# Reordering GpSimd's deviations, gathers and scatters in a two-layer cross-attention and expert kernel

## The reference

```python
x = x + tanh(g_xattn[0]) * L0_xattn(layernorm(x), ctx, ctx, ...)      # 16 heads of 8
x = x + tanh(g_ffn[0])   * L0_ffn(layernorm(x), ...)                  # 8 experts, the best 2 of each token, gelu
x = x + tanh(g_xattn[1]) * L1_xattn(ctx, ctx, layernorm(x), ...)      # 16 heads of 8
x = x + tanh(g_ffn[1])   * L1_ffn(layernorm(x), ...)                  # 4 experts, gates from logits and an entropy
```

## Time and profile before

| | |
|---|---|
| median of three runs | 1276.24 us |
| the profiled execution, its own time | 1273.86 us |
| its span, first to last instruction | 1272.1 us |
| PE busy | 1085.7 us (85%) |
| DVE busy | 905.7 us (71%) |
| ACT busy | 756.2 us (59%) |
| POOL busy | 543.2 us (43%) |

### The profile page before, as it was taken

How to read it: one execution, slowest core, us unless ns; L and a number is a source line. 1 busy time by engine, 2 the same in 40 slices (tenths; PEclk the granted TensorE clock), 3 DMA queues, 4 the chain that set the end, 5 groups by cost and what they waited for, 6 DMA issues and landing times.

```text
span 1272.1 us, 40209 instructions
## 1 busy us (share of the span) xinstructions
PE 1085.7 (85%) x13845; PEld 898.6 (71%) x13845; DVE 905.7 (71%) x3061; ACT 756.2 (59%) x1629; POOL 543.2 (43%) x699
## 2 busy tenths in 40 slices
PE   6788888887674599999998788888888878999998
PEld 3566666665553399999998566666665657999997
DVE  4677877776674745454453378888888887998887
ACT  4788777786672155555554376677776774444443
POOL 2114544555635434444444466556555531222220
PEclk7999999999997699999999799999999998999999
DMA  6222211111100233333333121111111100000000
GB/s 189 82 77 93 66 44 47 50 52 46 50 31 32 81 88 98 92 95 95 95 95 89 33 49 43 47 43 45 45 45 42 40 7 1 26 18 23 19 22 26
DMA packets 116781, 71.89 MB, mean 57 GB/s; under 512 B 51736, under 2 KB 105240, under 8 KB 116632
## 3 DMA queue, kind: packets, MB, share of 16 engines
q1 hardware_dynamic: 108440, 53.13, 15.2%
q0 software_dynamic: 8192, 16.79, 4.3%
HBM read 45.88 MB, written 22.94 MB: 54 GB/s over the span
## 4 chain that ended last, share of the span: by engine, by line
PE 44%; issue 23%; POOL 15%; DVE 13%; SPq 3%; DMA 1%; ACT 0%; DVEq 0%; POOLq 0%; another core or an unknown queue 0%; ACTq 0%
PE ps_m L1773 10%; POOL w1a L658 8%; PE ps_p L1658 4%; PE ps_m L1658 4%; POOL rs L587 4%; DVE mx L996 3%; PE ps_s L1759 3%; PE ps_s L1760 3%; PE ps_s L1761 3%; PE ps_s L1490 3%; PE ps_s L1646 2%; PE ps_s L1648 2%; PE ps_s L1647 2%; PE ps_s L1589 2%; DVE Pr L1002 2%
## 5 line engine op out<-in xcount | busy, mean ns | idle before, releaser
L727 ACT ACTIVATE PT<-ps_p 128x512 f32<-128x512 f32 x320 | 187.6, 596 | 61.3 <-PE ps_p L1548 28.2
L996 DVE TENSOR_REDUCE mx<-ps_s 128x8 f32<-128x512 f32 x256 | 169.0, 680 | 44.8 <-PE ps_s L1490 44.8
L658 POOL DMA_INDIRECT w1a<-louts,gi x128 | 125.6, 981 | 121.0 <-DVE mx L996 53.0
L811 ACT ACTIVATE Kbd<-ps_s,c 128x512 f32<-128x512 f32 x128 | 87.8, 688 | 113.4 <-PE ps_s L1648 113.1
L1533 PE MATMUL ps_p<-cst,Pr 128*128 128x128 f32 x1024 | 146.4, 277 | 0.8 <-DVE orow L1268 0.4
L576 POOL TENSOR_TENSOR spare<-spare 1x1 f32<-1x1 f32 x99 | 21.3, 215 | 291.9 <-DVE b1s L1351 151.7
L1773 PE MATMUL ps_m<-xn3T 128*128 128x128 f32 x1136 | 137.9, 275 | 0.0
L1773 PEld LDWEIGHTS ps_m<-xn3T 128*128 128x128 f32 x1136 | 132.7, 192 | 0.0
L877 ACT ACTIVATE xn3T<-ps_s,b1s 128x256 f32<-128x256 f32 x284 | 111.5, 474 | 26.2 <-PE ps_s L1761 26.1
L616 POOL DMA_INDIRECT lists<-xn3T,pos x80 | 78.7, 984 | 103.1 <-DVE mx L996 77.2
L1533 PEld LDWEIGHTS ps_p<-cst,Pr 128*128 128x128 f32 x1024 | 120.0, 144 | 2.3 <-issue 0.9
(11 more groups left out here) (221 smaller groups left out, 2710.4 us busy)
## 6 DMA issues: line engine op xcount, KB each, us to landing
xn3T<-lists SPq DMA_DIRECT2D x71, 128.0 KB, 2.1
louts<-xn3T SPq DMA_DIRECT2D x71, 128.0 KB, 1.8
ctxg<-in_ctxT SPq DMA_DIRECT2D x32, 256.0 KB
Kbd<-in_ctxT SPq DMA_DIRECT2D x512, 8.0 KB
out<-x SPq DMA_DIRECT2D x16, 256.0 KB, 2.3
w1a<-in_L_ffn_W SPq DMA_DIRECT2D x8, 256.0 KB, 3.0
w2a<-in_L_ffn_W SPq DMA_DIRECT2D x8, 256.0 KB, 3.9
Pr<-in_ctxT SPq DMA_DIRECT2D x16, 128.0 KB, 2.4
```

Of the source, the lines that this page charges most:

```text
L658: nc.gpsimd.indirect_dma_start(ysb[g.par][:, s_, t, :], None, louts, bass.IndirectOffsetOnAxis(ap=gi[g.par][:, c:c + 1], axis=0)).then_inc ...
L727: return nc.scalar.activation(dst, src, ACT.Copy)
L996: V.tensor_reduce(mx[g.par][:, q, :], per_key(ps_s[:, q, :]), AX, ALU.max).then_inc(max_done, 1)
```

## The change

It moves GpSimd's work within steps and rows between two steps; no instruction that computes is added or removed.

- In the second layer the third gather, `rows_moved(2)`, stands behind `inverse_deviations` and no longer waits for `sub_done`.
- In the first layer's steps 32 to 35 the deviations come first. Then step 32 waits for the end of the last group's product of probabilities and values (`pv_done`), and all of a step's scatters follow, without the waits for maxima, which have no group there anyway.
- The scatters of group 27 go from step 32 to step 33, so step 32 has four scatters instead of eight, and step 33 has twelve instead of eight.

```diff
-             32: ((26, 0, 1), (27, 0, 1)), 33: ((28, 0, 1), (29, 0, 1)), 34: ((30, 0, 1),), 35: ((31, 0, 1),)}
+             32: ((26, 0, 1),), 33: ((27, 0, 1), (28, 0, 1), (29, 0, 1)), 34: ((30, 0, 1),), 35: ((31, 0, 1),)}
...
+                if g.layer == 0 and g.k >= GROUPS:
+                    if have(-2):
+                        inverse_deviations(g)
+                    if g.k == GROUPS:
+                        pool.wait_ge(pv_done, g.plus(-1).count(4, 4))
+                    for n in range(4):
+                        rows_moved(n)
+                    return
                 if g.layer == 1 and have(4):
                     places(g.plus(4))
...
                 rows_moved(1)
-                if have(0):
-                    pool.wait_ge(sub_done, g.count(2, 2))
-                rows_moved(2)
+                if g.layer == 0:
+                    if have(0):
+                        pool.wait_ge(sub_done, g.count(2, 2))
+                    rows_moved(2)
                 if have(-2) or have(2):
                     inverse_deviations(g)
+                if g.layer == 1:
+                    rows_moved(2)
                 if have(-1) and not (g.layer == 0 and g.k > LATE_SUMS):
                     rows_plus_constant(g.plus(-1))
                 rows_moved(3)
```

## The result

| | before | after |
|---|---|---|
| median | 1275.84 us (4 runs, 1275.03 to 1279.92) | 1257.02 us (4 runs, 1254.87 to 1258.49) |
| the profiled execution, its own time | 1273.86 us | 1258.49 us |
| its span | 1272.1 us | 1256.7 us |

The ratio is 0.9847, 95% interval 0.9824 to 0.9869: 18.8 us less, where 29.0 were forecast. The time lies inside the range of the prediction (1241 to 1261 us) and 10 us above the 1247 us that were forecast.

What follows compares the result with a forecast made beforehand. DVE was taken to bound the second layer's step, its one hole awaiting POOL's rs; the router and zeros the first layer's end. 24 x 0.96 = 23.0 plus 6 gives 29.0 us off 1276.24: 1247 us, range 1241 to 1261.

Steps and rivals of the forecast that it cites:

- The hole in front of `normalise`: Second layer's step: DVE idles 1.11 us awaiting POOL's rs; moving the gather behind the deviations gains at least 0.62 us.
- That gives 0.34 us more: Second layer's step: a gather between rs and xc keeps xc off normalise, four taking 1.11 us instead of 1.45.
- The number of steps: Second layer: 24 of steps 2 to 27 gain 0.96 us each, 23.0 us; steps 0, 1, 24 and 25 left out.
- it doesn't do what it says: Rival, second layer: PE or the keys' loads set the step, the hole only moves; 0 to 6 us gained; chance 0.04.
- The first layer's end: Steps 32 to 35: unbroken product, rs and cnti over 12 us earlier, experts' gate opens 5.2 to 6.4 us earlier; 6 taken.
- If all under the scatters are slow, at 2.8 us each: First layer's end: seven zero fills issued while scatters run, the last landing near 430.8 us instead of 436.03.
- `normalise` isn't quickened: Rival, second layer: a step gains only 0.62 us, 21 us in all, 1255 us; chance 0.23 shared with xc in front.
- hold up the gate's hidden layer: Rival, second layer: xc delays line 1130 by 0.54 us; step gains 0.42, total 1260 us; chance 0.23 shared with unquickened normalise.
- Bunched gathers: Rival, second layer: four indirect DMAs in a row delay instructions, 2.09 us per step, 1297 us; chance 0.05.

Runs made afterwards that it cites:

- `l2_after_hold`: Kernel before plus only the second layer's part, with GpSimd waiting after the deviations for normalise before third gather and xc: ratio 0.9724, 1208.27 us beside 1243.58.
- `l2_gather_hold_xc`: Kernel before, second layer only: deviations, third gather, wait for normalise, xc, fourth gather; ratio 0.9689, 1206.12 us beside 1243.71.
- `l2_gathers_then_xc_clean`: Kernel before, second layer only: deviations, third gather, fourth gather, then xc, without an added wait; ratio 0.9709, 1207.65 us beside 1243.95.
- `l1_only`: Kernel before plus only the first layer's part of the change (steps 32 to 35 and the new scatter table): ratio 0.9989, 1241.62 us beside 1243.58.
- `l2_only`: Kernel before plus only the second layer's part of the change (third gather behind the deviations): ratio 0.9875, 1227.16 us beside 1243.58.

## Why the prediction was right, and where its sum was not

**The hole in front of `normalise`: right, and larger than I held for certain.** I took 0.62 us as the floor, from step 28, and allowed the power 1.16 us beside DVE's combine. It took 1.04, and `normalise` came 1.01 us earlier. By itself this part was sized too low.

**"That gives 0.34 us more": the step that failed.** It said that a gather between `rs` and `xc` keeps `xc` off `normalise`. By the records `xc` does start at its forecast place (858.46, 1.24 us after the power; 1.25 were forecast), yet two `normalise` lasted 0.42 us longer each. The term was -0.51 us instead of +0.34. `l2_after_hold` shows the mechanism behind it to be right: kept off, `normalise` takes 1.12 us, and the step gains more than the 0.96 forecast (10.18 to 8.94). `l2_gather_hold_xc` and `l2_gathers_then_xc_clean` show that `xc` is the one, not the gather: it costs more when it is queued one gather behind `rs` (0.84 us) than when it runs at once (0.34 us). How it meets the third, whose 751 ns (857.85 to 858.61) are nearly over at 858.46, isn't settled: GpSimd's spans are rough. The Trainium skill, "SBUF — State Buffer", section "Who interferes with whom", says that whoever issues first gets the shared port for a whole instruction and the other fully blocks. The traces agree for the first `normalise` in the kernel before and for the fourth in the change: each ends 0.09 us behind `xc` (875.54 and 875.45, 859.29 and 859.20). They don't for the third, which was issued 0.6 us before `xc`. The same section's starved descriptors are not seen: the gather takes 1.01 us under `normalise` and 0.94 to 0.98 elsewhere, and in both cases its packets start 0.7 us behind its end.

**The number of steps: right in size, with one term missing.** From step 2 to step 28 it is 12.7 us: 0.49 in each of most steps, 2.0 in steps 24 and 25 together, where ACT's idle of 2.09 us is down to 0.74, and 0.5 us lost in step 28, which lasts 10.06 us instead of 9.56. So steps 24 and 25, left out of the 24, gained as well. The other 2.4 us of the 15.1 come in steps 0 and 1, for which the prediction took nothing. PE, ACT and the loads didn't take the hole's place, as the rival "it doesn't do what it says" had it; PE still waits for the division, 1.24 us (timeline of PE, after):

```profile
860.37 0.41 PE L1473 MATMUL ps_m<-cst,On 128*128 128x128 f32 x2 [1.24 <-DVE On L1041]
```

**The first layer's end: the order of events was right, the gate was mis-sized.** The product whole, `rs` and `cnti` 12 to 14 us earlier: all as forecast. "If all under the scatters are slow, at 2.8 us each" was the case that came, but the fills were slower than that: they go out at 414.78, 418.35, 421.92, 426.85 and 433.15, that is 3.6, 3.6, 4.9 and 6.3 us apart, and four are out when the last scatter ends, not seven. So the zeros land at 437.98 instead of 430.8 plus the 4.3 us by which the product started late, 435.1. So the term was 2.4 us instead of 6. `l1_only` shows that even without slow fills it isn't 6: there the scatters' own end is the gate, 0.8 us earlier.

**The sum.** 15.1 + 2.4 with 1.5 less in the experts' stage and 0.7 behind step 28 is 19.7 us; the 4.3 us before the last product go off, and 15.4 are left, the difference of the spans. The medians differ by 18.8, since the profiled execution is 2.0 us below its median before and 1.5 above it after. That the time lies in the range owes something to luck: of the sum's terms that of `xc` had the wrong sign and that of the first layer's end came to less than half of its 6 us, and what made up for part of it wasn't in the sum: the hole gave 1.01 us instead of 0.62, and the layer's start 2.4. Of the rivals, "`normalise` isn't quickened" (1255 us) came out nearest, but by luck, not by its own road: the hole gave more than it said and `normalise` got slower. `xc` did not hold up the gate's hidden layer: line 1141 takes 0.28 us. Bunched gathers stopped nobody in the change: DVE is busy 9.52 of 9.69 us. In the three later kernels on the slower chip ACT's copy is late by 0.9 to 1.2 us in each step, much as that rival had it, and the steps still get shorter (9.24 to 9.51 us); whether the gathers are the cause isn't shown.

## What to carry to other kernels

A move that takes an instruction off the path also moves what stood behind it: price the followers at their new place, under each engine that may then be running. Here a GpSimd instruction that reads SBUF beside DVE's `tensor_scalar` was best put behind two DMAs or behind a wait for DVE; on the faster chips that was worth as much again as the change itself (`l2_only` has 0.9875, the kernels in which `xc` is away from `normalise` 0.9689 to 0.9724). Where a gate waits for several things, freeing the latest one gives only the distance to the next, so each must be timed from the same point.

## What the runs showed that was not expected

- The same kernel takes 1243.6 to 1244.0 us on three chips and 1276.8 us, 2.7% more, on a fourth, with a granted TensorE clock of 0.95 to 0.97 on all. On the slower one SP's instructions come in pieces of 0.70 us beside GpSimd's scatters, PE's product is broken up, and eight fills take 10.8 to 21.8 us; on the faster ones they take 8.1 to 8.2 us. Why is open.
- An indirect scatter takes 2.23 us from the start of its issue to its landing (0.96 of them the issue itself), more than the 1.71 us of a zero fill.
- A gather under four `normalise` costs DVE nothing (1.12 us for four), a `tensor_tensor` of 0.71 to 0.74 us costs it 0.34 or 0.84 us, depending on what stands in front of it.
